# Self-attention of a decoder layer on one core: stacked score operands, head buffers in device memory, an unrolled loop

## The reference

```python
qkv = jnp.einsum('bsd,od->bso', x, w_qkv) + b_qkv
q, k, v = jnp.split(qkv, 3, axis=-1)          # each (B, S, 32, 16)
scores = jnp.einsum('bqhd,bkhd->bhqk', q, k) * scale
alibi = slopes[:, None] * positions[None, :]   # a row per head, the same for every query
scores = jnp.where(causal, scores + alibi[None, :, None, :], -1e9)
attn = jax.nn.softmax(scores, axis=-1)
out = jnp.einsum('bhqk,bkhd->bqhd', attn, v).reshape(B, S, D)
return jnp.einsum('bsd,od->bso', out, w_out) + b_out
```

## Time and profile before

| | |
|---|---|
| median of 3 runs | 1065.37 us (1063.99 to 1065.83) |
| profiled execution, first to last instruction | 1065.3 us |
| PE, PEld, DVE, ACT, POOL busy | 93%, 77%, 72%, 47%, 41% |
| mean granted TensorE clock | 0.952 |
| stage A | 0 to 85.9 us |
| stage B up to the first output product | 85.9 to 144.9 us |
| stage B from there on | 144.9 to 277.9 us |
| stages C and D | 277.9 to 1065.3 us |

### The profile page before, as it was taken

One profiled execution on the slowest core, in us unless ns is written; L12 is line 12 of the kernel. 1 busy time (PEld: TensorE's weight loads), 2 busy tenths in 40 slices (PEclk: granted clock), 3 DMA queues, 4 the chain that ended last, 5 costly groups with the idle time before them and its releaser, 6 DMA issues. The chain is left out here.

```text
span 1065.3 us, 17470 instructions
## 1 busy us (share of the span) xinstructions
PE 987.9 (93%) x4940; PEld 825.1 (77%) x4940; DVE 765.2 (72%) x2345; ACT 503.1 (47%) x1581; POOL 437.0 (41%) x367
## 2 busy tenths in 40 slices
PE   6997999999778999999999999999999999789996
PEld 5875999999556887887887887787778777578885
DVE  4445568888697787777877877777777788784646
ACT  4325669898335435445345435444444435441220
POOL 1762000000357556546546646637546455340101
PEclk9997579999899999999999999999999999999998
DMA  8032212222221102002002002002001002210001
GB/s 298 1 99 60 60 37 59 46 58 70 87 82 50 40 11 65 31 5 69 30 0 76 22 0 79 20 0 79 20 15 64 10 18 73 78 62 10 30 1 39
DMA packets 41372, 52.02 MB, mean 49 GB/s; under 512 B 5104, under 2 KB 21616, under 8 KB 41200
## 3 DMA queue, kind: packets, MB, share of 16 engines
q1 hardware_dynamic: 41008, 50.44, 15.6%
q0 software_dynamic: 320, 1.05, 0.3%
HBM read 40.98 MB, written 2.10 MB: 40 GB/s over the span
## 5 line engine op out<-in xcount | busy, mean ns | idle before, releaser
L1060 POOL TENSOR_TENSOR C_t<-C_t 128x512 f32<-128x512 f32 x80 | 104.5, 1310 | 153.2 <-DVE C_t L965 153.2
L817 ACT ACTIVATE C_prob<-C_prob,C_ntop 128x128 f32<-128x128 f32 x256 | 99.8, 391 | 87.9 <-DVE C_ntop L997 87.8
L34 PE MATMUL C_yb<-C_woh,C_oh 128*128 128x512 f32 x256 | 107.5, 420 | 17.4 <-POOL C_wol L1088 12.3
L774 ACT ACTIVATE C_qh<-C_t 128x512 fp32r<-128x512 f32 x64 | 40.5, 633 | 141.0 <-POOL C_t L1060 141.0
L1010 DVE TENSOR_TENSOR C_ol<-C_ov,C_oh 128x512 fp32r<-128x512 f32 x64 | 44.2, 691 | 85.8 <-ACT C_oh L792 85.8
L34 PE MATMUL C_pj<-xTh,wh 128*128 128x512 f32 x256 | 101.3, 396 | 3.7 <-DVE xTl L128 2.2
L492 ACT ACTIVATE B_prob<-B_prob,B_ntop 128x128 f32<-128x128 f32 x256 | 99.2, 392 | 8.5 <-DVE B_ntop L573 7.3
L34 PE MATMUL C_yb<-C_woh,C_ol 128*128 128x512 f32 x256 | 102.8, 402 | 0.0
L34 PE MATMUL C_yb<-C_wol,C_oh 128*128 128x512 f32 x256 | 102.6, 401 | 0.0
L34 PE MATMUL C_pj<-xTh,wl 128*128 128x512 f32 x256 | 100.8, 394 | 0.0
L34 PE MATMUL C_pj<-xTl,wh 128*128 128x512 f32 x256 | 100.6, 393 | 0.0
(11 more groups left out here) (219 smaller groups left out, 2867.1 us busy)
## 6 DMA issues: line engine op xcount, KB each, us to landing
stage<-wq_dram SPq DMA_DIRECT2D x32, 256.0 KB, 3.4
stage<-wo_dram SPq DMA_DIRECT2D x32, 256.0 KB, 3.1
qs<-q SPq DMA_DIRECT2D x16, 256.0 KB, 2.7
kd<-k SPq DMA_DIRECT2D x128, 32.0 KB, 2.0
stage<-wqkvT_dram SPq DMA_DIRECT2D x10, 256.0 KB, 5.9
x<-x_nat_dram SPq DMA_DIRECT2D x1, 2048.0 KB, 10.1
stage<-wk_dram SPq DMA_DIRECT2D x8, 256.0 KB, 3.2
stage<-ctxT_dram SPq DMA_DIRECT2D x8, 256.0 KB, 3.0
```

Source lines behind the costliest of these rows:

```text
L34: mm = eng.matmul(out, stationary[i], moving[j], start=first and n == 0, stop=last and n == len(PASSES) - 1)
L817: last = eng.activation(e, e, ACT.Exp, bias=ntop[:, s % 2, h:h + 1], scale=1.0, accum_out=total[:, s % 2, h:h + 1])
L1060: eng.tensor_tensor(t1[:, j % 2, :], t1[:, j % 2, :], t2[:, j % 2, :], ALU.add).then_inc(s_sum, 1)
```

## The change

- The scores of two heads come from one matmul of 256 columns. The contraction holds, for each of the two heads, 16 rows of k-high by q-high, 16 of k-high by q-low, 16 of k-low by q-high, so that the three terms of the split are summed in the array. Two further rows of k hold the bias of the head in high and low part, against rows of ones in q. A group of four heads takes two matmuls instead of three of 512 columns.
- With the bias in the matmul, DVE adds one causal table of 128x128 for all heads. The eight tables aren't loaded; one table and a flat row of the bias are, and POOL prepares them.
- q and k no longer stay in SBUF. Each tile is split into a ring of three tiles (`tile_hl`) and stored to device memory, two DMAs of 256 KB for each tile. ACT's copy of tile i waits until tile i-3 has been stored.
- The operands of a half batch (`SelfHeads.load`) come from device memory in eight DMAs, rows of 512 bytes, 768 KB in all. Both halves of batch 0 are loaded in stage A, behind the store of tile 10 and ahead of that of tile 11.
- The weights of stage A get buffers of their own, and the zeroing of `kd` on DVE and POOL goes; POOL fills the new buffers at the start.
- Stage B is written out for all batches. Stage C's first pieces are loaded after the last scores.

```diff
+class SelfHeads:
+    RING = 3
+    PAIRS = HS // 4
...
+    def store(self, eng, i, m, half, tile):
+        where = (self.q_d if m < C else self.k_d)[4 * (m % C):4 * (m % C) + 4, :, :, :, half * HALF:(half + 1) * HALF]
+        for t in range(2):
+            eng.dma_start(where[:, :, t].rearrange("j s d n -> (j s) d n"), tile[:, t, :].bitcast(F32))\
+               .then_inc(self.s_store[i % self.RING], 16)
+
+    def load(self, eng, b, i):
+        pairs, tok = slice(self.PAIRS * i, self.PAIRS * (i + 1)), slice(b * S, (b + 1) * S)
+        both = lambda d, s: d[pairs, s, :, :, tok].rearrange("j t d n -> (t d) j n")
+        high = lambda d, s: d[pairs, s, 0, :, tok].rearrange("j d n -> d j n")
+        for s in range(2):
+            r, cols = 3 * DH * s, slice(s * S, (s + 1) * S)
+            for dst, src in ((self.q[i][r:r + 2 * DH, :, :], both(self.q_d, s)),
+                             (self.q[i][r + 2 * DH:r + 3 * DH, :, :], high(self.q_d, s)),
+                             (self.k[i][r:r + DH, :, cols], high(self.k_d, s)),
+                             (self.k[i][r + DH:r + 3 * DH, :, cols], both(self.k_d, s))):
+                eng.dma_start(dst.bitcast(F32), src).then_inc(self.s_load[i], 16)
...
-            for n in range(NG):
-                eng.dma_start(slots[n], alibi_d[:, n, :]).then_inc(s_alibi, 16)
-            load_heads(eng, 0, 0, q, k, qs, kd, s_load)
+            for i in range(QK):
+                kind, m, h = order[i]
+                eng.wait_ge(s_vhi, i + 1)
+                eng.wait_ge(s_vlo, i + 1)
+                heads.store(eng, i, m, h, tile_hl[:, i % heads.RING, :, :])
+                if i == QK // 2 + 2:
+                    heads.wait_stored(eng, QK // 2)
+                    for j in range(2):
+                        heads.load(eng, 0, j)
...
                 if kind == "qk":
-                    dst = (q if m < C else k)[:, 2 * (m % C), h * HALF:(h + 1) * HALF]
+                    if i >= heads.RING:
+                        eng.wait_ge(heads.s_store[i % heads.RING], 32 * (i // heads.RING))
+                    dst = tile_hl[:, i % heads.RING, 0, :]
...
-                if i == 4 * C:
-                    eng.memset(kd[:, 0:C, :, :].bitcast(F32), 0.0).then_inc(s_zero, 1)
...
-            for b in range(3):
+            for b in range(B + 1):
                 for G in range(NG):
                     step(b, G)
-            with eng.Fori(3, B) as b:
...
-            eng.wait_ge(s_top, NS - 3)
+            eng.wait_ge(s_sc, NS)
             for n in range(first.RING):
                 first.load(eng, n)
...
-                    c, cols = G // 2, slice(4 * (G % 2), 4 * (G % 2) + 4)
-                    product(eng, sc[G % 2][:, :].rearrange("p (h s) -> p h s", h=HG), [qs[:, 2 * c + j, :] for j in range(2)],
-                            [kd[:, 2 * c + j, cols, :] for j in range(2)], True, True).then_inc(s_sc, 1)
+                    for i in range(2):
+                        j = 2 * (G % PAIR) + i
+                        mm = eng.matmul(sc[G % 2][:, 2 * S * i:2 * S * (i + 1)], heads.q[G // PAIR][:, j, :],
+                                        heads.k[G // PAIR][:, j, :], start=True, stop=True)
+                    mm.then_inc(s_sc, 1)
...
-                            slots[G][:, h * S:(h + 1) * S], 1.0, -3e38, ALU.add, ALU.max, top[:, G % 2, h:h + 1])
+                            heads.causal[:, :], 1.0, -3e38, ALU.add, ALU.max, top[:, G % 2, h:h + 1])
```

More of the change, by code:

```diff
@@ L220, in project_self @@
     at = {p: n for n, p in enumerate(pieces)}
-    tiles = [("qk", m, h) for h, part in ((0, 0), (0, 1), (1, 0), (1, 1)) for m in range(part * C, part * C + C)] + \
+    order = [("qk", m, h) for h, part in ((0, 0), (0, 1), (1, 0), (1, 1)) for m in range(part * C, part * C + C)] + \
             [("v", b, 0) for b in range(B)]
-    order = tiles
+    QK = heads.TILES
     Q_DONE = 3 * C
@@ L229, in project_self @@
         xT = [sb("xT" + s, [P, C, NT], F32R) for s in ("h", "l")]
+        w = [sb("w" + s, [P, 2, C, D], F32R) for s in ("h", "l")]
+        rest = sb("rest", [P, RING - FirstPieces.RING, D])
+        slots = [stage[:, n, :] for n in range(FirstPieces.RING)] + \
+                [rest[:, n, :] for n in range(RING - FirstPieces.RING)]
         bout = sb("bout", [P, D])
@@ L420, in live @@
         def live(b, G, lag=0):
[L422 removed]
+            return 0 <= NG * b + G - lag < NS
         def follows(b):
[L426 removed]
+            return 1 <= b <= B
         def loop(eng, step):
[L430 removed]
+            for b in range(B + 1):
                 for G in range(NG):
                     step(b, G)
[L433 to L437 removed]
             step(B + 1, 0)
@@ L441, in _ @@
         def _(eng):
-            def load(b, pair):
-                eng.wait_ge(s_sc, NG * (b - 1) + PAIR * (pair + 1))
-                load_heads(eng, b, pair, q, k, qs, kd, s_load)
-            eng.wait_ge(s_zero, 2)
-            load_heads(eng, 0, 1, q, k, qs, kd, s_load)
-            for b in range(1, 3):
-                for pair in range(2):
-                    load(b, pair)
-            with eng.Fori(3, B) as b:
-                for pair in range(2):
-                    load(b, pair)
-            eng.wait_ge(s_top, NS - 3)
+            for b in range(1, B):
+                for i in range(2):
+                    eng.wait_ge(s_sc, NG * (b - 1) + PAIR * (i + 1))
+                    heads.load(eng, b, i)
+            eng.wait_ge(s_sc, NS)
             for n in range(first.RING):
```

117 lines of the change are left out of this document (65 added, 52 removed).

## The result

The changed kernel takes 1087.95 us (1085.62 to 1088.74) where the kernel before takes 1064.68 us (1062.39 to 1065.83) on the same chip: a ratio of 1.023, 95% interval 1.0182 to 1.0278. It is 2.3% slower. The forecast was 1060, with a range from 1047 to 1078.

The account below looks back on a forecast made before the run. TensorE was taken to bound stage B up to its first output product, TensorE and ACT to be level behind it. Terms -14 - 6 + 9 + 6 = -5 on 1065.3 gave 1060 us, range 1047 to 1078.

Parts of the forecast that it names:

- Point 2: Stage B up to the first output product: cheaper scores at clock 0.5 cut 56.7 us to 42.8, -14 us.
- The scores get no cheaper: Rival, stage B: a 256-column matmul with new weights costs what one of 512 does; 1066 us or more; chance 0.06.
- Point 3: Stage B behind the first product, clock high: ACT bounds steps at 2.01 us, a batch 18.45 instead of 19.25; -6 us.
- Point 4: Stage B behind the first product: clock low for 15 of 48 steps, +0.6 us each, +9 us (0 to +29).
- the two rivals: Clock behind stage B's first product: stays high (1051 us, chance 0.23), or low for most steps (1075 to 1080, chance 0.22).
- the second rival: Stage B: clock falls soon after each product, stays low until the next; 1075 us at 40 low steps; chance 0.22.
- Point 5: Stage A, SP's queue: issuing batch 0's sixteen loads holds SP 10.4 us, delaying later tiles; +6 us (+1.8 to +8).
- Point 6: Stage A, stores otherwise: a ring buffer is in use at most 7.6 of 8.2 us, hidden by TensorE's time.
- Point 7: Stage B, half-batch loads: issues and landing make 8.6 us, needed after 10 us at the fastest; hidden by 1.4 us.
- Half-batch loads come late: Rival, stage B: loads land in 6 us instead of 3.4 and TensorE waits; +14 us, 1074; chance 0.09.
- Point 8: Priced at nothing: zeroing of `kd`, alibi tables, POOL's fills at the start, unrolling, later load of stage C's first pieces.

## Why the prediction was wrong

**Point 2, up to the first product: right, as far as one profile of each can say.** -14.1 measured, -14 forecast, at a clock of 0.58. Against the execution of the same steps in which the clock rose early (55.0 us) it would be -10, so the agreement to 0.1 us is luck. Steps at the low clock take 2.90 us, forecast 2.93. Two matmuls of 256 columns cost 0.57 us at 0.5, taken from rows 7 as 0.6. "The scores get no cheaper" is out.

**Point 3, ACT's bound and the catching up: right.** A batch wholly at the high clock takes 18.40 us, forecast 18.45. Six batches at 18.4 would have been 110.4 us against 116.2 of before, -5.8 where -6 stood.

**Point 4, the low clock: right in kind, mis-sized.** The clock falls behind the products and the next one lifts it, as forecast, between the two rivals. The six batches from product to product took 282.37 - 151.01 = 131.36 us, 21.0 more than at the high clock, where +9 stood. Two sizes were off. A low step was priced at 0.6 us, 2.93 less a batch's average of 2.3; but that average holds the product, and the steps that fell low were the three at the end of a batch, which take 1.58, 1.76 and 2.62 us when the clock is high and 2.90 each when it is low. Outside their products the four batches in which it fell took 12.8 us more than four at the pace of the other two, 1.07 for each of their twelve whole low steps (15 were forecast). And the products themselves begin at the low clock: the product at 215.92 took 4.13 us and that at 193.99 took 2.87; over the five that begin low it is 8.1 us. The sum left them out; the second rival only mentioned them. The kernel with doubled scores puts the whole term to the test: its clock doesn't fall between the products and 17.3 of the stretch's 148.1 us go (130.8), although it does more.

**The Trainium skill's rule** ("TensorE: Matmul & The Clock Gate", HAM oscillation), by which gaps of idle time lose the clock and sustained work keeps it, is not enough here. The clock fell in stretches where TensorE was busy 96% of the time, and stayed low where it was busy 100% of it. The 48.90 of 48.90 us by which the prediction spoke against the rule were one execution, though; in another the clock did rise among the same steps, at 133.7 us.

**Point 5, SP's queue in stage A: right place, price too small.** The prediction had the copy of tile 14 at 60.7; it came at 74.37, 13.7 late. Of these, 6.0 are that SP reached the store of tile 11 at 63.49 and not at 57.5. The issue of the loads took no longer than priced (9.5 against 10.4 us); SP came late to it because the tiles were late, 6.3 us by tile 10, behind slow stores. The other 7.7 are that the store let the copy go 10.9 us after it was issued instead of 3.2. The kernel with wide stores, which has as many bytes of loads in the same place, separates this point from the next: there SP reached the store of tile 11 at 57.52 and the copy came at 62.85, 2.1 late. So of the 13.7 us, 2.1 are this point's own error and 11.6 go with the slow stores: 6.0 on the way to SP's issue and 5.6 between the issue and the copy. The clock had a share too: the prediction allowed 1 us for the time at the low clock behind the wait, and the rows give some 3. The step of this point that failed: it counted what the sixteen loads cost the *issuing* queue and nothing for their 1.5 MB, which move through the same DMA engines ahead of the store. Rows 10 gave a landing in 2.0 us for a store with nothing else under way.

**Point 6, stores otherwise: wrong, and the larger error in stage A.** It bounded a landing by 2 to 3.4 us and found the ring covered, 7.6 of 8.2 us. But a store is two DMAs, laid out as 8 by 16 rows, and these run at half of the DMA engines, about 190 GB/s; ACT's copies waited 36.1 us for stores where 0 stood, 22.8 of them outside the wait behind the loads. With the loads out of the way such stores leave stage A 7.3 us longer than before, and 8.4 longer than wide stores do (93.2 against 84.8). With wide stores and the loads left in their place stage A is 8.8 us over before where +6 was forecast, so 11.4 of the 14 us of error in stage A go with this point. The diff showed it: the outermost dimension of the destination is 8. The Trainium skill ("DMA: Bandwidth & Descriptors", Rules for kernel authors, the row to use all 16 engines) says that an outermost dimension of fewer than 16 keeps a whole DMA on at most so many engines. The trace agrees: a share of 0.5 and some 190 GB/s with 8 outermost, 0.9 and up to 413 GB/s with 128. The prediction didn't weigh it.

**Point 7, half-batch loads: right.** They landed in 3.3 us (forecast 3.4), and TensorE waits for none of them in stage B. "Half-batch loads come late" is out.

**Point 8: right.** C and D 787.5 us; the loop written out alone 0.9989.

Two slips in the prediction's arithmetic change nothing: 0.30 and 0.23 make 0.53 and not 0.54, and with loads issued in 0.4 us the copy of tile 14 would be 1.3 us late by the same steps, where +1.8 stood.

## What to carry to other kernels

When a change adds DMAs, put a price on three things apart: the issue on the queue, the bytes that stand ahead of what you wait for, and how many DMA engines its outermost dimension lets it use. When it makes TensorE's work cheaper in a kernel that is not bound by TensorE, ask what held the clock up before: here scores with a third of the columns saved 14 us ahead of the first product and lost 15 behind it, and issuing the matmuls twice, in time in which TensorE would otherwise have waited for ACT, was faster than issuing them once. Price a fall of the clock by the steps that really fall, with the dense products that follow them.

## What was not expected

- Filling TensorE's time with thin matmuls cost the clock: 147.1 us low instead of 66.2, 1115 us instead of 1069, with TensorE and its weight loads both busy 24.60 of 24.60 us.
- Loads of 512-byte rows from device memory moved slowly in stage A, with many under way: 134 GB/s at a DMA share of 1.04. Issued last, with no store behind them, the sixteen moved 1.59 MB in some 10.5 us and still came in time for stage B. Whether it is their number, the place of the rows in device memory, or the tiles having been written just before was not tried.
- The clock, once lifted in batches 0 and 1, is lost in 10 to 17 us although the scores are doubled there too; from the third batch on, where each batch also has an output product, it holds. This stays open.
